# A graph layer on one core: projection and vectors on ScalarE's queue, turned ahead of the edge search, and a flag read between two products

## The reference, cut to what matters

```python
h = relu(layernorm(x))
xn = batchnorm(h, g1, b1)
agg = segment_sum(xn[src], dst) / max(degree, 1)
conv_out = relu(agg @ W_conv + b_conv)
q, k, v = heads(h[:256] @ Wq), heads(h[:256] @ Wk), heads(h[:256] @ Wv)
# 8 heads of 64; random features phi through proj (256 x 64)
qf, kf = phi(q), phi(k)
attn = (qf @ (kf.T @ v)) / (qf @ kf.sum() + KEPS) @ Wo   # rows past 255 take row 255
out = x + batchnorm(conv_out + attn + h, g2, b2)
```

## Time and profile before

| what | value |
|---|---|
| median of 3 runs | 175.11 us (174.8 to 175.3) |
| profiled execution, own time | 174.95 us |
| its span, first to last instruction | 173.1 us |
| busy: PE, PEld, DVE, ACT, POOL | 166.0, 109.6, 138.3, 89.8, 7.6 us |

### The profile page before, as it was taken

How to read it: one execution, slowest core, us unless ns; L and a number is a source line. 1 busy time by engine, 2 the same in 40 slices (tenths; PEclk the granted TensorE clock), 3 DMA queues, 4 the chain that set the end, 5 groups by cost and what they waited for, 6 DMA issues and landing times.

```text
span 173.1 us, 3035 instructions
## 1 busy us (share of the span) xinstructions
PE 166.0 (96%) x1135; PEld 109.6 (63%) x1136; DVE 138.3 (80%) x317; ACT 89.8 (52%) x163; POOL 7.6 (4%) x22
## 2 busy tenths in 40 slices
PE   7999999999999999999999999999999999999980
PEld 2588887545545546557767797684464574777960
DVE  3987989899947786999656785976999998597980
ACT  3228998749793789969506164218600505004060
POOL 5047000000000000000000000000000000000000
PEclk9999999999999999999999999999999999999996
DMA  5999960000800000000000000000395004050046
GB/s 169 353 342 284 310 221 0 0 4 0 251 12 0 4 0 0 0 4 2 0 4 0 0 4 0 0 4 4 94 315 187 0 27 121 6 146 2 0 118 183
DMA packets 12412, 13.71 MB, mean 79 GB/s; under 512 B 1474, under 2 KB 7788, under 8 KB 12396
## 3 DMA queue, kind: packets, MB, share of 16 engines
q1 hardware_dynamic: 11116, 12.18, 22.4%
q10 hardware_dynamic: 960, 1.05, 1.8%
q0 software_dynamic: 320, 0.26, 0.7%
HBM read 10.92 MB, written 2.56 MB: 78 GB/s over the span
## 4 chain that ended last, share of the span: by engine, by line
PE 88%; DVE 6%; ACT 2%; issue 1%; DVEq 0%; ACTq 0%
PE bank L992 22%; PE bank L715 20%; PE bank L645 8%; PE bank L666 4%; PE bank L739 4%; PE bank L729 4%; PE bank L758 4%; PE bank L797 4%; PE bank L692 4%; PE bank L657 3%; PE bank L637 3%; PE bank L703 2%; PE bank L1020 2%; DVE r L1412 1%; DVE r L1407 1%
## 5 line engine op out<-in xcount | busy, mean ns | idle before, releaser
L992 PE MATMUL bank<-r,gh 128*128 128x512 f16 (+8 forms) x140 | 39.3, 314 | 0.0
L992 PE MATMUL bank<-r,gl 128*128 128x512 f16 (+8 forms) x140 | 39.3, 313 | 0.0
L715 PE MATMUL bank<-wc,xs 128*128 128x512 f32 (+1 forms) x80 | 38.5, 608 | 0.2 <-DVE gl L1243 0.2
L1100 DVE TENSOR_TENSOR ohb<-iota,bcol 128x1280 f16<-128x1280 f16 x25 | 20.5, 819 | 3.7 <-PE bank L657 3.7
L715 PEld LDWEIGHTS bank<-wc,xs 128*128 128x128 f32 (+1 forms) x80 | 13.6, 187 | 11.6 <-issue 11.6
L398 ACT ACTIVATE r<-bank 128x500 f16<-128x500 f32 x25 | 18.3, 765 | 3.4 <-PE bank L657 3.4
L992 PEld LDWEIGHTS bank<-r,gh 128*128 128x128 f16 (+1 forms) x140 | 13.5, 97 | 8.5 <-issue 0.3
L992 PEld LDWEIGHTS bank<-r,gl 128*128 128x128 f16 (+1 forms) x140 | 13.6, 97 | 8.2
L613 ACT ACTIVATE bw<-mv,epst 128x1 f32<-128x1 f32 x4 | 1.2, 295 | 31.0 <-DVE mv L1418 31.0
L645 PE MATMUL bank<-hT,r 128*128 128x256 f32 x64 | 14.6, 383 | 0.0
L657 PEld LDWEIGHTS bank<-ohv,ohb 128*128 128x128 f16 x250 | 9.7, 98 | 6.6 <-issue 5.3
(11 more groups left out here) (179 smaller groups left out, 269.1 us busy)
## 6 DMA issues: line engine op xcount, KB each, us to landing
xs<-in_x SPq DMA_DIRECT2D x15, 256.0 KB, 5.0
out<-xs SPq DMA_DIRECT2D x7, 256.0 KB
r<-in_L_gnn_Wq SPq DMA_DIRECT2D x2, 512.0 KB, 7.2
r<-in_L_gnn_Wk SPq DMA_DIRECT2D x1, 1024.0 KB, 5.6
wc<-in_L_gnn_W_conv SPq DMA_DIRECT2D x1, 1024.0 KB, 9.6
wvo<-in_L_gnn_Wv SPq DMA_DIRECT2D x1, 1024.0 KB, 12.8
wvo<-in_L_gnn_Wo SPq DMA_DIRECT2D x1, 1024.0 KB, 5.2
xs<-in_x ACTq DMA_DIRECT2D x3, 256.0 KB, 4.4
```

Source lines behind the costliest of these rows:

```text
L715: last = nc.tensor.matmul(acc[0:n, :], xnT[:, f, i * P:i * P + n], wc[:, f, :], start=(f == 0), stop=(f == FT - 1))
L992: last = nc.tensor.matmul(acc[:, 0:cn], gg[0:n, s, f * P:(f + 1) * P], A16[0:n, s, c0:c0 + cn], start=(s == 0 and gg is gh), stop=(s == NT ...
L1100: last = V.tensor_tensor(oh[:, s0:s0 + n, :].rearrange("p s (m t) -> p s m t", t=2), iota16[:, 0:size].rearrange("p (m t) -> p m t", t=2). ...
```

## The change

Four things change:

- The five vectors and the two halves of the projection are issued on ScalarE's queue behind tile 1; tiles 3 and 5 go from there to Sync's queue, ahead of tiles 2 and 4.
- `project_consts` runs right behind the first dummies, before `edge_search(0)`, and there are 15 dummies instead of 18. `("consts",)` moves to the head of the bank order, so the steps ahead of `("k", 0)` take the next bank each.
- ScalarE instead of VectorE copies the turned bank to `pT` and `vec`, behind its two first copies of `hT`. VectorE's `constants` waits for that.
- TensorE waits for the flag and reads it between the two output products; the branch stays behind the second.

```diff
--- before.py
+++ after.py
@@ -42,7 +42,7 @@
 NPAD = NT * P
 SLOW_LINKS = 8
 SEARCHED = 2
-ROUSE, ROUSE_NEXT = 18, 1
+ROUSE, ROUSE_NEXT = 15, 1
 EP, EJ = 125, E // 125
 XN_MAX = 37.0
 EXP_MASK = 0x7F800000
@@ -189,8 +189,8 @@
         V_G1, V_B1, V_G2, V_B2, V_BC = range(5)
 
 
-        order = [("first",), ("hT", 1), ("hT", 0), ("q", 0), ("q", 1), ("hT", 2), ("hT", 3), ("hT", 4), ("hT", 5),
-                 ("consts",), ("k", 0), ("hT", 6), ("hT", 7), ("hT", 8), ("hT", 9), ("dq",), ("k", 1), ("uk", 0), ("uk", 1),
+        order = [("consts",), ("first",), ("hT", 1), ("hT", 0), ("q", 0), ("q", 1), ("hT", 2), ("hT", 3), ("hT", 4), ("hT", 5),
+                 ("k", 0), ("hT", 6), ("hT", 7), ("hT", 8), ("hT", 9), ("dq",), ("k", 1), ("uk", 0), ("uk", 1),
                  ("wsum",), ("cols",), ("dqT",), ("uk", 2), ("uk", 3), ("v", 0), ("uk", 4), ("uk", 5), ("v", 1), ("uk", 6),
                  ("uk", 7), ("uq", 0), ("uq", 1), ("G", 0), ("cinv",), ("dk",), ("G", 1), ("qfT", 0), ("qfT", 1), ("dkT",),
                  ("uq", 2), ("uq", 3), ("kmaxT",), ("G", 2), ("qfT", 2), ("qfT", 3), ("kmax",), ("uq", 4), ("uq", 5),
@@ -315,17 +315,13 @@
             sp.dma_start(edst[:, :], dst.rearrange("(p j) -> p j", p=EP)).then_inc(dst_in, 16)
             wq_rows = w_q.rearrange("(t p) n -> p t n", p=P)
             sp.dma_start(wq[:, :, 0:2 * P], wq_rows[:, :, 0:2 * P]).then_inc(wq_in[0], 16)
-            load_x(2)
-            load_x(4)
+            for i in (3, 5, 2, 4):
+                load_x(i)
             sp.dma_start(wq[:, :, 2 * P:D], wq_rows[:, :, 2 * P:D]).then_inc(wq_in[1], 16)
             for i in (6, 7, 8, 9):
                 if i == NT - 1:
                     sp.wait_ge(pad_zero, 1)
                 load_x(i)
-            for k, v in enumerate((g1, b1, g2, b2, b_conv)):
-                sp.dma_start(vrow[4 * k:4 * k + 4, :], v.rearrange("(t p) -> t p", p=P)).then_inc(vec_in, 16)
-            for k in range(2):
-                sp.dma_start(pj[:, :, k * DH:(k + 1) * DH], proj.rearrange("(t p) d -> p t d", p=P)).then_inc(pj_in, 16)
             sp.wait_ge(x_in[7], 16)
             sp.dma_start(wk, w_k.rearrange("(t p) n -> p t n", p=P)).then_inc(wk_in, 16)
             sp.dma_start(wc[:, :, :], w_conv.rearrange("(t p) n -> p t n", p=P)).then_inc(wc_in, 16)
@@ -425,8 +421,11 @@
                 act.wait_ge(ln_var, gi + 1)
                 act.activation(lnw[:, 1, a:b], mv[:, a:b, 1], ACT.Sqrt, bias=epst[:, 0:1]).then_inc(ln_std, 1)
 
-            for i in (1, 3, 5):
-                act.dma_start(xs[:, i, :], x[i * P:(i + 1) * P, :]).then_inc(x_in[i], 16)
+            act.dma_start(xs[:, 1, :], x[P:2 * P, :]).then_inc(x_in[1], 16)
+            for k, v in enumerate((g1, b1, g2, b2, b_conv)):
+                act.dma_start(vrow[4 * k:4 * k + 4, :], v.rearrange("(t p) -> t p", p=P)).then_inc(vec_in, 16)
+            for k in range(2):
+                act.dma_start(pj[:, :, k * DH:(k + 1) * DH], proj.rearrange("(t p) d -> p t d", p=P)).then_inc(pj_in, 16)
             act.wait_ge(cst_set, 7)
             act.activation(early[:, :], epst[:, :], ACT.Sqrt)
             ln_std_of(0)
@@ -434,6 +433,9 @@
             ln_tile(0)
             store_hT(1, ACT.Relu)
             store_hT(0)
+            acc = landed(act, "consts")
+            act.activation(pT[:, :], acc[:, 0:M], ACT.Copy)
+            act.activation(vec[:, :], acc[:, M:M + 20], ACT.Copy).then_inc(read("consts"), 1)
             ln_std_of(1)
             act.wait_ge(ln_ready, 2)
             ln_tile(2)
@@ -759,9 +761,7 @@
                                                 start=(c == 0), stop=(c == FT - 1))
                 last.then_inc(full("ha", i), 1)
 
-            def uncovered_edges():
-                pe.wait_ge(flag_ready, 1)
-                covered = pe.value_load(flag[0:1, 0:1], min_val=0, max_val=1)
+            def uncovered_edges(covered):
                 with pe.If(covered == 0):
                     for i in range(NT):
                         stored(pe, "G", i)
@@ -855,8 +855,9 @@
                 nc.tensor.matmul(acc[:, 0:HEADS], ones[0:HEADS, :], dg8[:, :], start=True, stop=True).then_inc(full("kmax"), 1)
 
             rouse(ROUSE)
+            pe.wait_ge(id_set, 1)
+            project_consts()
             edge_search(0)
-            pe.wait_ge(id_set, 1)
             transpose_h(1)
             transpose_h(0)
             rouse(ROUSE_NEXT)
@@ -871,7 +872,6 @@
             transpose_h(3)
             transpose_h(4)
             transpose_h(5)
-            project_consts()
             pe.wait_ge(wk_in, 16)
             qk("k", wk, 0)
             transpose_h(6)
@@ -978,8 +978,10 @@
             for i in range(2):
                 stored(pe, "attnT", i)
             heads_out(0)
+            pe.wait_ge(flag_ready, 1)
+            covered = pe.value_load(flag[0:1, 0:1], min_val=0, max_val=1)
             heads_out(1)
-            uncovered_edges()
+            uncovered_edges(covered)
             assert counts[0] == NGRP
 
             def aggregate(f, c):
@@ -1139,9 +1141,6 @@
                                 ALU.mult).then_inc(read("q", i), 1)
 
             def constants():
-                acc = landed(dve, "consts")
-                V.tensor_copy(pT[:, :], acc[:, 0:M])
-                V.tensor_copy(vec[:, :], acc[:, M:M + 20]).then_inc(read("consts"), 1)
                 stored(dve, "consts")
                 gv1, bv1 = vec[:, 4 * V_G1:4 * V_G1 + 4], vec[:, 4 * V_B1:4 * V_B1 + 4]
                 V.scalar_tensor_tensor(out=xb[:, 0, :], in0=gv1, scalar=-1.0, in1=gv1, op0=ALU.mult, op1=ALU.max)
```

## The result

The changed kernel takes 183.87 us (183.6 to 184.21, four runs) against 175.11: a ratio of 1.0503 (1.048 to 1.0527). The forecast was 174.3, in a range up to 175.4. The profiled execution took 183.6 us around a span of 181.6, 8.5 more than before.

What follows compares the result with a forecast made beforehand. TensorE, busy for 166.0 us of a 173.1 us span, was taken to bound the kernel. The terms -0.65 + 0.39 + 0.35 - 0.48 + 0.10 - 0.34 = -0.63 turned 174.95 into 174.3 us, range 173.8 to 175.4.

Steps and rivals of the forecast that it cites:

- when the data land: TensorE behind the dummies: projection lands at 7.3, 3.9 us after issue, dummies end at 6.95; +0.35 us (0 to 2.85).
- Rival C: Projection lands late, from 7.93 on, and TensorE's wait outgrows the gains: 175.6 half way, 176.8 at worst; chance 0.16.
- rival D: TensorE's clock falls back after fewer dummies and a wait; work before the old turning at most doubles: 186; chance 0.02.
- The dummies: Start of TensorE's work: fifteen dummies end at 6.95 instead of eighteen at 7.61; -0.65 us.
- The old turning: TensorE before the first key product: the turning's time from 18.57 to 19.05 goes; -0.48 us.
- The new turning: TensorE right behind the dummies: three transposes hold the array; +0.39 us, if the data are there.
- ScalarE: Longer issues delay its first layer-norm use by nothing or up to 0.3 us; its two copies fall into idle time.
- The key weights: Ahead of the key products: weights land at 18.1 to 18.6, TensorE arrives at 18.66; +0.1 us (0 to 0.3).
- The transfers' spread: Tiles 3 and 5 on Sync's queue: costs nothing, or a tenth or two where tile 3 is late.
- The flag read: Between the output products: the branch's fetch begins earlier, the gap before the degree sums goes; -0.34 us (0 to -0.34).
- Rival B: The branch waits for the array, so moving the flag read does nothing: -0.29 us in all, 174.7; chance 0.20.

Runs made afterwards that it cites:

- held-back run: Changed kernel, with Sync issuing tiles 3, 5, 2, 4 and all that follows only once the projection has landed: 180.0 us in one run.
- run with the projection first: Changed kernel, with the projection's two halves issued ahead of the five vectors on ScalarE's queue: 180.2 us in one run.
- single-wait run: Kernel before, with one added TensorE wait for tile 6 of x between the 18 dummies and the edge search: 183.09 us, ratio 1.0438.
- 40-dummy run: Changed kernel with 40 dummies instead of 15 and nothing else: 179.19 us, ratio 1.0203.

## Why the prediction was wrong

The step that failed is **when the data land**. I took 3.9 us after issue, from tiles on the same queue, with a worst case of 6.4; it was 7.9. The term was +0.35 (0 to 2.85); the wait was 5.25, of which 0.55 is that the dummies ended at 6.40 instead of 6.95. I priced what was ahead by bytes, 74 KB. The chain and the queues show that five vectors of 2 KB held the queue to about 7, and that the projection's rows then took until 11 beside Sync's traffic. The held-back run puts a number on the traffic: 3.9 instead of 7.9 for the second half, with the vectors still ahead. The run with the projection first puts one on the vectors: 7.1 instead of 7.9, or 2.7 with the time that their issues take. So the traffic of the other queue was the larger part.

The second error is one of **independence**. Rival C (late data) and rival D (the clock) had 0.16 and 0.02 as separate cases; C's worst, 176.8, had no lower clock in it, and D's bound, 186, no late landing. The single-wait run shows that D follows from C. Each hole from 1.77 us up that a profile shows (1.77, 3.34, 4.60, 5.25) was followed by the lower clock, and those of 0.65 and 0.88 were not. That is one execution each, with the rise at different instants, so it gives no limit. I argued against D with a gap of 0.34, from a place with a different past and a fifteenth of the length. The 40-dummy run gave back 4.7 us of the 8.8. The Trainium skill's sentence on transposes ("TensorE: Matmul & The Clock Gate", Part 4) pointed at the right danger by a mechanism that isn't needed: with the added wait alone the clock fell before a transpose had run, and with 27 or 40 dummies the same transposes followed without a fall.

The other terms. *The dummies*, -0.65: nothing that can be told from 0 by themselves, as the run with three fewer shows (0.9987 to 1.0029); the array then waits for tile 1, and the 7.61 that I took for the dummies' end isn't steady either (below). With data on time the early turning could at best have been free, in the 0.65 that the array then waits anyway, and the change worth its old place and the flag, by my estimate some 0.9 us (0.38 and 0.51); no run shows this. *The old turning*, -0.48: 0.38 by the chain, from the last transpose of tile 5 to the first key product. *The new turning*, +0.39: 0.88, at the lower clock. *ScalarE*: its root was 0.3 late (5.90), the bound I had given, and hidden by the wait; with only the transfers moved, where no wait hides it, it cost nothing either. *The key weights*, +0.1: TensorE came so late that they had long landed, so this was not tested in the change. *The transfers' spread*: nothing, as forecast (0.9998), but for the one run of 179.25. *The flag read*, -0.34: right in mechanism, 0.51 in the chain and 0.3% alone. The part beyond 0.34 is in the degree sums, 0.53 instead of 0.69; I take it that the sequencer, once ahead, also gets through its waits before them, but no run shows that apart. Rival B falls: the branch took 3.50 in the changed kernel and 3.70 with the flag read alone, and ended before the output products did. What "Runtime: NRT & Kernel Launch" (Instruction fetch mechanics) of the Trainium skill says of taken branches agrees with the one page fetched in each.

## What to carry to other kernels

Work that stands in for warm-up work has to be there as surely as the warm-up work was: data that arrive late cost TensorE the wait and then the clock, here 5 us and another 4.4. Before moving a load, count the transfers ahead of it on its queue and the traffic beside it, and not only the bytes ahead. Then put the work where its data are surely there (174.89 here); dummies up to the latest likely landing save the clock but not the delay (176.11). The register read that feeds the branch stood 16 products ahead of it here at no cost, and let the branch end before the array did.

## What was unexpected

- The instant at which the clock rises scatters. Eighteen dummies from 1.21 took 6.56 us in the kernel before, 5.46 in the run with the wait for tile 6 and 6.93 in that with the wait for the queries' weights; fifteen took 5.19, 5.54, 5.57 and 5.94. Between executions of nearly the same start, the end of eighteen dummies differs by 1.5 us, more than the change hoped to gain.
- After the hole of 5.25 the lower level held for 10.2 us, 11.65 to 21.9, through work without a gap. Behind the hole of 4.60 it held as long, behind those of 1.77 and 3.34 for 6.8; the lengths are not explained by any run here.
- A wait for a transfer, 1.8 us long, can cost 4 us: 180.2 in one run against 176.1 with twelve dummies more.
- Five transfers of 2 KB on one queue held what was behind them for three microseconds, 3.9 to 7.0, beside a loaded queue. Whether that is a turn taken per transfer or a slow start of each was not separated.
